# A two-layer decoder kernel: split first load and unread products, context products behind the experts, an earlier second gather

## What is computed

```
x = norm(x + attention0(x))              # 16 heads of 64, causal
x = norm(x + cross0(x, ctx))             # one head of 256
x = norm(x + experts(x))                 # 8 experts of 512, the best 2 of each token
x = norm(x + block1(x))                  # 16 heads of 16: gated, clocked, rotated attention, out_w, gelu MLP
x = norm(x + cross1(x, ctx, ctx))        # 4 heads of 64: keys = ctx Wk^T, values = ctx Wv^T, Wp
x = norm(x + mixer(x))                   # receptance, key, value products with shifted tokens
```

```
q, k, v = (split_heads(a, W) for a, W in ((x, Wq), (ctx, Wk), (ctx, Wv)))
attn = softmax(q k^T / 8 + causal);  out = (attn v) Wp^T + bp
```

## Time and profile before

| | us |
|---|---|
| median of three runs (1229.84 to 1233.21) | 1233.13 |
| the profiled execution | 1236.84 |
| its span | 1235.1 |
| TensorE busy | 1099.2 (89%), 6750 matmuls |
| VectorE busy | 725.8 (59%) |
| ScalarE busy | 543.2 (44%) |
| GpSimd busy | 461.5 (37%) |
| DMA | 52.38 MB, mean 42 GB/s |

### The profile page before, as it was taken

One profiled execution on the slowest core, in us unless ns is written; L12 is line 12 of the kernel. 1 busy time (PEld: TensorE's weight loads), 2 busy tenths in 40 slices (PEclk: granted clock), 3 DMA queues, 4 the chain that ended last, 5 costly groups with the idle time before them and its releaser, 6 DMA issues. The chain is left out here.

```text
span 1235.1 us, 20364 instructions
## 1 busy us (share of the span) xinstructions
PE 1099.2 (89%) x6750; PEld 793.1 (64%) x6750; DVE 725.8 (59%) x2212; ACT 543.2 (44%) x1379; POOL 461.5 (37%) x539
## 2 busy tenths in 40 slices
PE   7899989998999887799999948589898899899996
PEld 3476557545744676699999935355665575576874
DVE  1382366247525834456556547649849786966456
ACT  1381256227322821333333318357566657743551
POOL 0170034006300974566666635304522432323022
PEclk9999999999999998899999979679999999999999
DMA  6000200020002032651111114100100100000001
GB/s 202 18 2 1 59 18 2 0 58 19 1 0 59 2 113 73 242 178 53 44 53 50 46 52 145 35 1 1 35 9 1 35 10 18 1 2 26 1 1 35
DMA packets 40227, 52.38 MB, mean 42 GB/s; under 512 B 10780, under 2 KB 33372, under 8 KB 40124
## 3 DMA queue, kind: packets, MB, share of 16 engines
q1 hardware_dynamic: 31100, 36.66, 9.4%
q0 software_dynamic: 3408, 9.31, 2.7%
q10 hardware_dynamic: 5616, 5.11, 1.3%
HBM read 41.76 MB, written 9.31 MB: 41 GB/s over the span
## 5 line engine op out<-in xcount | busy, mean ns | idle before, releaser
L1682 PE MATMUL bank<-words 128*128 128x256 f32 (+3 forms) x872 | 266.9, 456 | 16.9 <-ACT words L2286 3.4
L1682 PEld LDWEIGHTS bank<-words 128*128 128x128 f32 (+1 forms) x872 | 162.1, 193 | 95.0 <-issue 56.1
L445 PE MATMUL bank<-words 128*128 128x512 f32 x384 | 173.0, 602 | 8.4 <-DMA words<-in_wq 8.4
L397 POOL TENSOR_TENSOR words<-words 128x256 f32<-128x256 f32 (+1 forms) x128 | 102.7, 833 | 155.2 <-DVE words L1016 154.7
L1219 PEld LDWEIGHTS bank<-words 128*128 128x128 f32 x1248 | 146.5, 193 | 3.5 <-ACT words L1253 1.6
L1219 PE MATMUL bank<-words 128*128 128x128 f32 x1248 | 147.0, 276 | 0.9 <-ACT words L1253 0.9
L445 PEld LDWEIGHTS bank<-words 128*128 128x128 f32 x384 | 72.5, 193 | 90.6 <-issue 90.3
L739 ACT ACTIVATE words<-words 128x128 f32<-128x128 f32 (+1 forms) x256 | 112.8, 444 | 30.6 <-DVE words L854 30.6
L731 ACT ACTIVATE words<-bank 128x512 f32<-128x512 f32 x48 | 28.7, 598 | 193.5 <-PE bank L445 193.5
L1268 ACT ACTIVATE words<-words 128x1024 f32 x39 | 41.1, 1057 | 144.3 <-PE bank L1219 112.8
L844 DVE COPY words<-bank 128x512 f32<-128x512 f32 x48 | 33.2, 691 | 106.7 <-PE bank L445 106.4
(11 more groups left out here) (346 smaller groups left out, 1983.7 us busy)
## 6 DMA issues: line engine op xcount, KB each, us to landing
words<-in_w SPq DMA_DIRECT2D x8, 1024.0 KB, 8.9
y_slots<-words ACTq DMA_DIRECT2D x39, 128.0 KB
words<-in_w SPq DMA_DIRECT2D x8, 512.0 KB, 9.4
words<-in_xt SPq DMA_DIRECT2D x4, 512.0 KB, 3.9
words<-in_x SPq DMA_DIRECT2D x4, 512.0 KB, 4.2
x_rows<-words SPq DMA_DIRECT2D x16, 128.0 KB, 1.8
words<-in_wm SPq DMA_DIRECT2D x2, 1024.0 KB, 6.7
out_x<-words SPq DMA_DIRECT2D x16, 128.0 KB, 1.8
```

The lines of the kernel that those rows point to most:

```text
L397: last = pool.tensor_tensor(part, part, inv[:, j % SLOTS0, :, t:t + 1].to_broadcast([P, 2, P * (t + 1)]), ALU.mult)
L445: last = pe.matmul(bank[c % 2][:, :], w, r, start=k == 0, stop=k == KD - 1)
L1682: last = pe.matmul(out, w, r, start=i == 0, stop=i == len(pairs) - 1)
```

## The change

Four things are put in together.

1. *First load.* x transposed is issued by ScalarE; SyncE issues the first 256 of 1024 query columns, then the rest. TensorE waits for the rest before chunk 2. The transposed context has a layout of features by all tokens, so a group's part is one DMA and not two.
2. *Unread products.* VectorE fills a tile with ones, and TensorE multiplies it five times with itself (128x128 by 128x256) before its first wait. Nobody reads the result.
3. *Context products.* The experts' block also loads wxk, wxv and the context of three groups. At the opening of the last layers TensorE computes keys and values of groups 0 to 2 (16 matmul instructions each), ScalarE copies them into the MLP's still empty buffer, SyncE stores them to DRAM, and loads each group's back ahead of its use. In the periods the products, copies and context loads go. The last group's stay in the tail.
4. *Second gather.* Group 1's rows go into `zxt` and `x5t`, which are empty then, and GpSimd issues the gather between its additions for the two halves. The zeroing of a column of `x5t` goes behind it.

```diff
@@ attention_layers, sync
-            load_x(0)
-            for dst, src, done in ((wq, dram["wq0"], qweights), (wk, dram["wk0"], kweights), ...
+            load_queries(slice(0, FIRSTQ), qweights)
+            load_queries(slice(FIRSTQ, E0), restqueries)
+            for dst, src, done in ((wk, dram["wk0"], kweights), ...
@@ attention_layers, tensor
+                if g == 0 and c == FIRSTQ // P:
+                    pe.wait_ge(restqueries, 16)
...
+            pe.wait_ge(filled, 1)
+            for n in range(5):
+                pe.matmul(bank[2][:, 0:S], x1[:, 0, 0:P], x1[:, 0, :], start=True, stop=True)
             pe.wait_ge(const, 1)
@@ attention_layers, scalar
+            act.dma_start(xt[:, :, :], dram["xt"].rearrange("(k p) n -> p k n", p=P)[:, :, 0:GT]).then_inc(xloaded, 16)
@@ attention_layers, vector
+            dve.memset(x1[:, 0, :], 1.0).then_inc(filled, 1)
@@ expert_layer, sync, behind the other early loads
+            for part, name in zip(keep["l_ctx"], ("wxk", "wxv", "ctxt")):
+                sp.dma_start(part[:, :, :], dram[name].rearrange("(k p) n -> p k n", p=P)[:, :, 0:part.shape[2]]).then_inc(keep["ctx"], 16)
@@ last_layers, sync
+            for g in range(G - 1):
+                sp.wait_ge(ckr, 2 * g + 2)
+                sp.dma_start(dram["kx"][g], keptk[:, g, :]).then_inc(cstored, 16)
+                sp.dma_start(dram["vx"][g], keptv[:, g, :]).then_inc(cstored, 16)
             sp.wait_ge(n3.stats, 2)
...
+                if z is not None:
+                    load_context(z + 1)
@@ last_layers, gpsimd
+                pool.wait_ge(ckr, 2 * (G - 1))
                 pool.memset(va[:, :, :, :], 0.0)
...
                     pool.tensor_tensor(firstrb[:, t, :], firstrb[:, t, :], firstra[:, t, :], ALU.add).then_inc(swung, 1)
-            pool.wait_ge(vmm, NT)
-            gather(1)
+                if b == 0:
+                    gather(1)
@@ last_layers, tensor
+            def context_rows(g):
+
+                firstk, firstv, firstmem = keep["l_ctx"]
+                for c in range(KD):
+                    last = product(bank[2 * g][:, c * GB * S2:(c + 1) * GB * S2],
+                                   [(firstk[:, k, tok(c)], firstmem[:, k, bass.ts(g, GB * S2)]) for k in range(KD)])
+                last.then_inc(ckm, 1)
                 for b in range(GB):
...
+            pe.wait_ge(keep["ctx"], 3 * 16)
+            for g in range(G - 1):
+                context_rows(g)
             pe.wait_ge(early, NE1 * 16)
...
                     pe.wait_ge(xqr, KD * z + KD)
+                    pe.wait_ge(cloaded, 32 * z + 32)
                     context_scores(z, 0)
...
-                    pe.wait_ge(loaded, 32 * r + 32)
-                    context_keys(r, 0)
-                    context_keys(r, 1)
                     weighted(a, QUADS1 - 1)
                     if a + 1 < G:
                         turn_front(a + 1)
-                    context_values(r)
@@ last_layers, scalar
+            for g in range(G - 1):
+                act.wait_ge(ckm, 2 * g + 1)
+                act.activation(keptk[:, g, :], bank[2 * g][:, 0:KD * GB * S2], ACT.Copy).then_inc(ckr, 1)
+                act.wait_ge(ckm, 2 * g + 2)
+                act.activation(keptv[:, g, :], bank[2 * g + 1][0:S2, 0:GB * D], ACT.Copy).then_inc(ckr, 1)
             front_rows(0, 0)
...
+                    if r == 0:
+                        act.wait_ge(cstored, 16 * 2 * (G - 1))
                     for c in range(4):
                         gelu(r, c)
...
-                if r is not None:
-                    keys_copy(r, 0)
-                    keys_copy(r, 1)
...
-                    if r is not None:
-                        values_copy(r, b)
```

## The result

The changed kernel takes 1221.56 us in the median (1220.46 to 1224.23, 4 runs) beside 1233.17 us of the kernel before (4 runs): a ratio of 0.9919, 95% interval 0.9894 to 0.9945. Timed again later beside 18 runs of the kernel before it came to 0.9915, 0.9883 to 0.9947. The forecast was 1221.0. The number held, in part by luck: 3.2 us of the forecast stood for a pause that is no property of the kernel, the start gave 0.8 us less than I had, and the context products gave 2.5 us more in the traces, which made up for most of the two.

The account below looks back on a forecast made before the run. TensorE, busy for 89% of 1235.1 us, was taken as the bound. Terms -2.3 - 2.5 + 0.3 - 2.2 - 2.0 - 0.3 - 3.2 = -12.2 us gave 1224.6 for the profiled execution, 1221 for the median; range 1214.5 to 1229.

Parts of the forecast that it names:

- First load: At the start, x and fewer query weights land at 6.1 us: 2.3 us gained, between 1.4 and 2.7.
- Unread products: At the start, ten matmuls under the load raise TensorE's clock earlier: 2.5 us gained, between 0 and 3.1.
- The pause: VectorE's 3.76 us stand before 795.99, laid to the second group's old gather: 3.2 us gained, between 0 and 3.8.
- Rival 1: In the last layers' first attention, the pause isn't the gather's, or it moves: gain 9.0 us, 1224; chance 0.20.
- The base: Sums were made against the profiled execution, 1236.84 us; its 3.7 us above the median of 1233.13 were carried over unchanged.
- The gap: After the experts, 48 context matmuls take 10.2 us, nearly all covered: +0.3 us, between -0.5 and +6.2.
- First boundary: Between periods, forms at 906.77: exponentials hide the keys; values and copies give 2.0 us, between 1.0 and 2.2.
- Second: Period boundary with forms at 1017.64: they could start about 1015.1; 2.2 us gained, between 1.2 and 2.8.
- Third: Period boundary where VectorE divides at 1125.10 without idle time before: TensorE's saving lost, 0.3 us gained, between 0 and 1.
- My limit, VectorE's division: At the boundary with forms at 1017.64, VectorE's division for the older group, at 1016.39, can come only 1.2 us earlier.
- The gather's new place: Issued before GpSimd's second-half additions, the gather costs nothing, with 4.5 us left; at worst 0.1 to 0.6 us late.
- The slower rival: TensorE stays at 1.2 GHz into the first group's attention after the experts: 23.8 us more, 1245; chance 0.06.

## Why the prediction was right in number, and where it wasn't

- *First load*, -2.3: first products at 8.06 to 8.37 without and 6.10 to 6.49 with the split, so 2.0 in the mean. Right.
- *Unread products*, -2.5: 2.0 between the means of the step to 29.8 (20.8 and 18.8). The price read from the profiled execution, 21.44, was the longest of six; the three other traces of the old start have 20.0 to 20.75. A size off by half a microsecond, for the reason of the next point too: one execution was taken for the kernel.
- *The pause*, -3.2: wrong. The step that failed is "the pause of 3.76 us lay in the old gather". I had seen it beside a gather twice in one execution and took that for a cause. Rival 1 was right that it wasn't the gather's; that it would stay was wrong too.
- *The base*: I carried the 3.7 us between the profiled execution and the median over unchanged. The pause was 3.3 us of that execution (20.55 against 17.25 in the second one), so the median had never held it, and nothing could be taken off the median for it. The sum without it is -9.0, or 1224.1.
- *The gap*, +0.3: 107.3 to 107.4 us from 721 to 832 in the changed kernel against 107.0 to 107.1. Right in sum, with two shifts in it that I didn't have: the burst was 1.7 us longer, the turning of the second half's rows came 0.3 to 0.5 later and the work at 752.6 was 0.8 to 1.1 later, and from there to 832 the traces are 0.5 to 0.9 shorter. In the kernel with the context products alone it is +1.0.
- *First boundary*, -2.0: 14.88 to 12.59, so -2.3, in eight of ten traces; -0.9 in the two others, which had 3.4 us at 1.2 GHz there. *Second*, -2.2: -2.9 in all ten. My limit, VectorE's division, didn't hold: it runs at 1002.09, after the forms have begun, so the forms don't wait for it. *Third*, -0.3: in all ten the stretch from 1110 to 1125 is 1.9 us shorter (13.0 for 14.9) and the one from there to 1139.5 at least 1.9 longer (16.4 or more for 14.5), so TensorE's saving is given back, as I had it. In sum 0 in three of ten traces, and 0.9 longer in seven, which had 3.4 us at 1.2 GHz there, as none of the four without the products had.
- *Not foreseen*: from 1200 to 1221, 0.9 us less in eight of ten traces and 0.2 and 1.0 more in the two others; all four without the products had some 2 us at 1.2 GHz there, the eight none, the two 3.4 and 5.0. From 1221 to the end nine of ten are 0.6 to 0.7 shorter as well. From 971 to 1087 two of the four without the products lose 1.5 us to such a moment, and a third, the one with the gather moved, 1.6 us at another place; none of the ten with them does (below). The first trace's 0.5 us from 971 to 985 has no time at 1.2 GHz; the second pause lies there.
- *The gather's new place*: 0, as costed. The issues were 0.1 us longer in the mean (0.95 to 1.25 us), and the addition behind them was done at 767.25; VectorE read its result at 772.15. The warning that I had drawn from the Trainium skill ("SBUF — State Buffer", section "Who interferes with whom") rests there on VectorE's two-port modes, which shut GpSimd out; tensor_tensor has none of them, and with two inputs in SBUF it holds up GpSimd's reads alone. VectorE's instructions beside the issues were mostly tensor_tensor, scans and reductions, so this case hardly tests it.
- *The slower rival* didn't come: the clock was at 1.2 GHz for parts of the burst and again from 734 to 736, and was back at 1.00 from 738; it is low again for most of 765 to 815, as it is before.

So the start is worth about -4.0 us where I had -4.8, the gather nothing where I had -3.2, and the context products more than the -4.2 that I had for them. From 721 to the end, three traces without these products and without the pause take 510.1 to 510.3 us, and eight with them (all but the two with added products in this part) 502.1 to 506.2, in the mean 503.5: -6.7. With the start that makes 10.7, inside the 10 to 12 that the whole was timed at. The forecast of 12.2 was reached as -4.8 - 4.2 - 3.2, the traces have it as -4.0 - 6.7 and nothing: the mechanism of the first two terms was right, though a part of the 6.7 (the clock's moments from 971 to 1087 and from 1200 on) wasn't foreseen, the third was wrong, and that the sum came out near is luck. One thing doesn't fit: timed alone the context products gave -3.4 (interval 0.7 to 5.2), though their one trace gives -6.5 from 721 on. That stays open.

## What to carry to other kernels

A wait that the profile can't name is worth a second profile of the same kernel before it is worth a term in a sum: of fourteen executions one had it. Compare traces by the lengths of stretches between the same instructions: most repeat within 0.1 us, which no timing of whole runs can resolve, and for those that don't, look first at how long TensorE stood at its lower clock in each. A sum of several terms that comes out right doesn't show that the terms are right; price them one by one. Work moved into a gap is free only until the gap is full; here the next ten microseconds cost 9.6 in the trace.

## What the runs showed of the hardware

TensorE's clock falls to 1.2 GHz for a moment between long stretches at 2.4 GHz, in some executions and not in others. The stretch that the table calls 971 to 985 shows it. Windows of the same instructions in the kernel before (second execution) and in the one with the gather moved; in each, first 3 us ahead and then the stretch from the start of one matmul to the start of the ninth behind it:

```profile
960.06:963.06 3.00, 1.10 (x9) 0.89 (x9) 3.00 (x5) 2.53 (x5) 2.23 (x3) 1.00 0.00 0
963.56:967.19 3.63, 3.63 (x10) 2.90 (x9) 3.47 (x10) 0.77 (x2) 2.76 (x3) 0.53 0.34 108
```

```profile
961.25:964.25 3.00, 1.10 (x9) 0.89 (x9) 3.00 (x5) 2.54 (x5) 2.23 (x3) 1.00 0.00 0
964.75:966.70 1.95, 1.95 (x11) 1.71 (x10) 1.79 (x5) 0.77 (x2) 1.65 (x2) 1.00 0.41 107
```

The nine matmuls take 3.63 us at a granted clock of 0.53 and 1.95 us at 1.00 (a window counts one that it only touches, too), and this makes the stretch 1.5 us longer (14.99 and 13.45). Ahead of them TensorE was busy for 1.10 of 3.00 us in both, so a light stretch ahead doesn't by itself decide whether the clock falls. The same happens near 1213:

```profile
1213.00:1216.00 3.00, 3.00 (x7) 2.45 (x8) 1.97 (x8) 0.00 (x0) 1.47 (x4) 0.50 0.00 0
```

Each costs 0.9 to 1.7 us where the table shows it. They are a part of the scatter of 2 to 12 us between the fastest and the slowest run of one kernel, and a change that moves TensorE's pauses moves them too: the third boundary has one in seven of ten traces with the context products in the gap and in none of four without. The Trainium skill ("TensorE: Matmul & The Clock Gate", section "What's actually happening") says that the number of slow matmuls at a kernel's start differs from run to run; the start here shows it (20.02 to 21.44 us for the same work), and it happens later in the kernel as well. From 450 to 470, in the last group's cross attention ahead of the experts, the same work took 16.4 to 16.7 us in traces with no time at 1.2 GHz, 18.0 to 18.3 with 3.4 us, and 19.7 to 20.0 with 6.8 (the eight traces of the table). The granted clock there was 0.84 and 0.69 over 450 to 455 and 460 to 465 in the second execution of the kernel before, 1.00 and 1.00 in the kernel with the context products alone.
